# Second batch's transposes and projections moved from turn 0 into the lead, and the SyncE queue of the lead reordered

## What is computed

```python
mod = (silu(c) @ wmod).reshape(4, 6, 1, -1)
sa, ca, ga, sb, cb, gb = (mod[:, n] for n in range(6))      # ga, gb kept away from zero
h = layernorm(x) * (1 + ca) + sa
xq, xk, xv = h @ wq.T, h @ wk.T, h @ wv.T                   # 16 heads of 16
probs = softmax(xq @ xk.T)                                  # over 512 keys, per head
x = x + ga * ((probs @ xv) @ wo.T)
h = layernorm(x) * (1 + cb) + sb
x = x + gb * moe(h)                                         # 32 experts, the best 4 of each token, and a shared one
```

## Time and profile before

| | us |
|---|---|
| median of 3 runs | 596.38 |
| lowest, highest | 596.19, 599.55 |
| the profiled execution | 599.47 |
| its span, first to last instruction | 597.7 |
| TensorE busy | 560.9 (94%) |
| VectorE busy | 374.9 (63%) |
| ScalarE busy | 255.3 (43%) |
| GpSimd busy | 206.1 (34%) |

### The profile page before, as it was taken

The page is one execution under the profiler, slowest core; times in us unless marked ns, Lnnn a source line. Parts: engine busy times, 40 slices in busy tenths (PEclk is TensorE's granted clock), DMA queues, the critical chain, the costliest instruction groups (busy, mean ns, idle before and its releaser), DMA issues.

```text
span 597.7 us, 10693 instructions
## 1 busy us (share of the span) xinstructions
PE 560.9 (94%) x3102; PEld 308.7 (52%) x3103; DVE 374.9 (63%) x888; ACT 255.3 (43%) x519; POOL 206.1 (34%) x268
## 2 busy tenths in 40 slices
PE   4989999999999999999999998989998999999983
PEld 3443323233333333333343455638887898988572
DVE  6375577778679786798856469545343443442588
ACT  3112635664866648555568240123333343444000
POOL 6200000000020751207533663722665666667200
PEclk9975999999999999999999999999999999999998
DMA  6133117100221222212100688433544655540592
GB/s 228 40 110 123 27 34 218 34 7 16 68 49 37 80 82 77 44 35 82 62 1 29 222 255 249 136 91 107 157 146 137 180 161 159 166 125 18 209 404 91
DMA packets 44119, 67.18 MB, mean 112 GB/s; under 512 B 9499, under 2 KB 32420, under 8 KB 43692
## 3 DMA queue, kind: packets, MB, share of 16 engines
q1 hardware_dynamic: 31984, 45.62, 26.5%
q0 software_dynamic: 7680, 16.87, 8.1%
q10 hardware_dynamic: 4416, 4.20, 2.1%
HBM read 38.93 MB, written 27.51 MB: 111 GB/s over the span
## 4 chain that ended last, share of the span: by engine, by line
PE 83%; DVE 9%; DMA 2%; issue 2%; SPq 2%; ACT 1%; POOL 0%; ACTq 0%; DVEq 0%; POOLq 0%
PE ps L875 23%; PE ps L888 11%; PE ps L1106 9%; PE ps L972 8%; PE ps L1127 6%; PE ps L824 5%; PE ps L966 4%; PE ps L1092 3%; PE ps L846 3%; PE ps L833 3%; PE ps L901 3%; DVE max_q L1217 2%; PE ps L1117 2%; PE ps L810 2%; PE ps L931 1%
## 5 line engine op out<-in xcount | busy, mean ns | idle before, releaser
L1217 DVE TENSOR_REDUCE max_q<-ps 128x1 f32<-128x512 f32 x256 | 163.7, 684 | 73.6 <-PE ps L846 71.7
L703 ACT ACTIVATE probs<-ps 128x512 f32<-128x512 f32 x256 | 138.0, 596 | 102.1 <-PE ps L875 101.8
L846 PE MATMUL ps<-k_rows,q_rows 31*128 31x512 f32 x512 | 150.1, 681 | 1.1 <-DMA k_rows<-qk_raw 1.1
L875 PE MATMUL ps<-q_rows,k_rows 32*128 32x512 f32 x512 | 146.4, 650 | 0.9 <-DVE max_q L1217 0.9
L561 POOL DMA_INDIRECT results<-y_sb,dest x96 | 94.9, 988 | 70.3 <-ACT y_sb L752 35.2
L875 PEld LDWEIGHTS ps<-q_rows,k_rows 32*128 32x128 f32 x512 | 41.8, 186 | 70.6 <-ACT probs L703 51.1
L1106 PE MATMUL ps<-up_sb,oT 128*128 x384 | 70.8, 327 | 0.9 <-issue 0.7
L888 PE MATMUL ps<-probs,v_ext 128*32 128x512 f32 x512 | 68.2, 605 | 1.1 <-ACT probs L703 1.1
L1106 PEld LDWEIGHTS ps<-up_sb,oT 128*128 128x128 f32 x384 | 61.3, 190 | 1.9 <-issue 1.8
L1579 DVE COPY oT<-ps 128x512 f32<-128x512 f32 x48 | 33.1, 691 | 32.8 <-PE ps L1092 32.8
L1127 PE MATMUL ps<-down_sb,e_hidT 96*128 x192 | 49.8, 382 | 4.0 <-ACT e_hidT L760 4.0
(11 more groups left out here) (181 smaller groups left out, 681.9 us busy)
## 6 DMA issues: line engine op xcount, KB each, us to landing
xe<-dispatched SPq DMA_DIRECT2D x96, 129.0 KB, 2.1
comb<-results SPq DMA_DIRECT2D x16, 512.0 KB, 10.6
up_sb<-in_up SPq DMA_DIRECT2D x12, 512.0 KB, 4.7
dispatched<-pad_rows SPq DMA_DIRECT2D x33, 129.0 KB, 4.0
down_sb<-in_down SPq DMA_DIRECT2D x4, 768.0 KB, 6.7
x<-in_x ACTq DMA_DIRECT2D x4, 512.0 KB, 4.8
q_rows<-qk_raw SPq DMA_DIRECT2D x64, 32.0 KB, 1.9
k_rows<-qk_raw SPq DMA_DIRECT2D x64, 32.0 KB, 1.9
```

The costliest lines, as they stand in the source:

```text
L703: act.activation(probs[:, u % 8, :], ps[:, st_bank(t.b, g, u), :], ACT.Exp).then_inc(exp_done, 1)
L846: pe.matmul(ps[:, banks[u % len(banks)], :], q_rows[32 * i:32 * i + ONE, b % 2, g, qt * P:(qt + 1) * P], k_rows[32 * i:32 * i + ONE, b % 2 ...
L875: pe.matmul(ps[:, st_bank(b, g, n), :], k_rows[32 * i:32 * i + 32, b % 2, g, kt * P:(kt + 1) * P], q_rows[32 * i:32 * i + 32, b % 2, g, :] ...
L1217: dve.tensor_reduce(max_q[:, g % 2, qt, i:i + 1], ps[:, banks[(16 * g + n) % len(banks)], :], AXX, ALU.max).then_inc(max_done, 1)
```

## The change

In the lead, TensorE now does TP0 and TP1 of batch 1 after score n = 11 of group 0 (both named with a +), QK0+ to QK3+ after n = 3, 7, 11 and 15 of group 1, and V0+ and V1+ behind them, before it waits for the 32 maxima. ScalarE's evacuations move with them, and the normalisation of batch 1 stands before `values_out` of batch 0; the VectorE instruction that it needs (`minus_mean_over_deviation`) moves ahead of the first maxima. TP, QK and V leave table FIRST; MAX3 stands at place 24 instead of 26. On SyncE, `max_rows(lead, 3)` goes in front of the three loads, the 32 placing DMAs of batch 1 go between the two sets of three loads, and turn 0 places nothing. scoreT of unit 2 waits for V0+. `done_in` lets later code find the lead's uses under turn 0.

```diff
@@ -57,10 +57,9 @@
 
 
 
-    LEAD = ("TP0", "TP1", "QK0", "QK1", "QK2", "QK3", "V0", "V1", "MAX3")
-
-    FIRST = {"MAX0": 0, "TP0": 1, "TP1": 3, "QK0": 5, "QK1": 7, "MAX1": 8, "MOD0": 9, "MOD1": 11, "V0": (13, 15),
-             "MAX2": 16, "MODT": 17, "QK2": (19, 21), "QK3": (23, 25), "MAX3": 26, "V1": (27, 29), "NT0": 30, "NT1": 31}
+    LEAD = ("TP0", "TP1", "QK0", "QK1", "QK2", "QK3", "V0", "V1", "TP0+", "TP1+", "MAX3", "QK0+", "QK1+", "QK2+", "QK3+", "V0+", "V1+")
+
+    FIRST = {"MAX0": 0, "MAX1": 8, "MOD0": 9, "MOD1": 11, "MAX2": 16, "MODT": 17, "MAX3": 24, "NT0": 30, "NT1": 31}
 
     MIDDLE = {"MAX0": 0, "QK0": 1, "WO0": 3, "WO1": 5, "QK1": (7, 9), "MAX1": 10, "V0": (11, 13), "HT0": 14, "HT1": 15,
               "MAX2": 16, "LOG": 17, "QK2": (19, 21), "QK3": 23, "MAX3": 24, "RANK": 25, "V1": (27, 29), "NT0": 30, "NT1": 31}
@@ -90,6 +89,13 @@
                     if self.fill and places[0] >= 16:
                         half = 1 - half
                     self.take(name, half, used)
+
+    def done_in(self, lead):
+
+
+        for name, use in lead.uses.items():
+            if name.endswith("+"):
+                self.uses[name[:-1]] = use
 
     def at(self, name, place):
 
@@ -285,6 +291,7 @@
         used = [0] * len(MISC)
         lead = Turn(-1, {"pre"}, used)
         turns = [Turn(0, {"att", "pre", "mod", "next"}, used)]
+        turns[0].done_in(lead)
         for b in range(1, B):
             turns.append(Turn(b, {"att", "post", "fill"} if b == B - 1 else {"att", "pre", "post"} if b == B - 2 else
                               {"att", "pre", "post", "next"}, used))
@@ -384,12 +391,9 @@
             def turn(t):
 
                 max_rows(t, 0)
-                if t.pre:
+                if t.pre and not t.mod:
                     place_rows(t, 0, 0)
                     place_rows(t, 0, 1)
-                if t.mod:
-                    place_rows(t, 1, 0)
-                    place_rows(t, 1, 1)
                 max_rows(t, 1)
                 if t.mod:
                     modulation_out()
@@ -399,10 +403,11 @@
                 if t.pre:
                     pad(11 * t.b, 11 * t.b + 11)
                 max_rows(t, 2)
-                if t.pre:
+                if t.pre and not t.mod:
                     for c in (2, 3):
                         for g in (2, 3):
                             place_rows(t, c, g)
+                if t.pre:
                     max_rows(t, 3)
 
             sp.wait_ge(consts, 3)
@@ -412,10 +417,13 @@
             for g in range(NG):
                 for c in range(2):
                     place_rows(lead, 2 * (g // 2) + c, g)
+            max_rows(lead, 3)
             sp.dma_start(wmod[:, :, 2 * D:6 * D], wmod_in[:, 2 * D:6 * D].rearrange("(k p) n -> p k n", p=P)).then_inc(w_ld, 16)
             for w_d, w_s in ((wo, wo_sb), (gate, gate_sb)):
                 sp.dma_start(w_s[:, :, :], w_d.rearrange("(k p) n -> p k n", p=P)).then_inc(w_ld, 16)
-            max_rows(lead, 3)
+            for c in range(4):
+                for g in (c // 2 * 2, c // 2 * 2 + 1):
+                    place_rows(turns[0], c, g)
             for w_d, w_s in ((sgate, sgate_sb), (sup, sup_sb), (sdown, sdown_sb)):
                 sp.dma_start(w_s[:, :, :], w_d.rearrange("(k p) n -> p k n", p=P)).then_inc(sh_ld, 16)
             for t in turns:
@@ -725,11 +733,17 @@
                 to_hT(lead, f"TP{k}", 0)
             for c in range(4):
                 raw_qk(lead, c)
+            act.wait_ge(nmr_s, 2)
+            normalise(turns[0])
             for m in range(2):
                 values_out(lead, m)
+            for k in range(KD):
+                to_hT(turns[0], f"TP{k}", 1)
             negate_max(lead, 3)
-            act.wait_ge(nmr_s, 2)
-            normalise(turns[0])
+            for c in range(4):
+                raw_qk(turns[0], c)
+            for m in range(2):
+                values_out(turns[0], m)
             for t in turns:
                 turn(t)
             finish(fin)
@@ -870,7 +884,7 @@
                 else:
                     if b == 0 and u == 2:
 
-                        written(pe, lead, "V1")
+                        written(pe, lead, "V0+")
                     above(pe, exp_done, 64 * b + u - 2)
                 pe.matmul(ps[:, st_bank(b, g, n), :], k_rows[32 * i:32 * i + 32, b % 2, g, kt * P:(kt + 1) * P],
                           q_rows[32 * i:32 * i + 32, b % 2, g, :], start=True, stop=True, tile_position=(32 * i, 0)).then_inc(st_full, 1)
@@ -1059,9 +1073,16 @@
                 score(0, 0, n, SC + ST[0:2])
                 if n in (3, 7):
                     project_v(lead, n // 4)
+                if n == 11:
+                    for k in range(KD):
+                        tokens_to_columns(turns[0], f"TP{k}", 1)
             turn_max(lead, 3)
             for n in range(16):
                 score(0, 1, n, SC + ST[0:2])
+                if n % 4 == 3:
+                    project_qk(turns[0], n // 4)
+            for m in range(2):
+                project_v(turns[0], m)
 
             pe.wait_ge(max_done, 32)
             pe.wait_ge(ones_ld, 16)
@@ -1562,9 +1583,9 @@
             for to, of in ((iota_ef, iota_e), (base_f, base_i), (thr_f, thr_i), (tile_f, tile_i)):
                 st.did(dve.tensor_copy(to[:, :], of[:, :]))
             st.did(dve.tensor_copy(tails[:, :, :, 0], home[:, :].rearrange("p (t k) -> p t k", k=TOPK)))
+            minus_mean_over_deviation(TJ, NT, 2)
             for n in range(16):
                 score_max(0, 0, n, SC + ST[0:2])
-            minus_mean_over_deviation(TJ, NT, 2)
             for n in range(16):
                 score_max(0, 1, n, SC + ST[0:2])
             for t in turns:
```

## The result

| | before | after |
|---|---|---|
| median | 597.20 us (20 runs) | 600.75 us (20 runs) |
| lowest, highest | 594.05, 601.37 | 597.12, 603.68 |
| ratio, 95% interval | | 1.0046 (1.0027 to 1.0066) |
| profiled execution, its span | 599.47, 597.7 | 600.14, 598.4 |

The ratio makes the changed kernel 2.7 us slower (1.6 to 3.9): within 1%, but clear of zero. The forecast was +0.7. It was made on the median of the 3 runs then shown; over more runs the median of the kernel before is 0.8 higher. The two medians of the table lie 3.6 apart; I go by the ratio. The 600.75 lies outside the forecast's own range (595.5 to 598.5), inside the wide one (593 to 602), and next to the 601.2 of rival (b).

The account below looks back on a forecast made before the run. TensorE, busy 94% of the span, was taken to bound the kernel, with VectorE bounding lead group 1; +2.15 up to place 8 and -1.41 after gave +0.7 on 596.38, so 597.1 us, own range 595.5 to 598.5, wide 593 to 602.

Parts of the forecast that it names:

- rival (b): SyncE's queue: placings and 1.5 MB of weights delay place 8's maxima to about 77, 4.1 late: 601.2 us; chance 0.2.
- transposed maxima of the lead (TP0+, TP1+ cost 0): End of group 0: two transposes of 0.59 us each hide under about four VectorE maxima and cost 0.
- low clock in the lead: Group 1: the clock falls as before, 6.5 to 8.0 us at half clock, losing 3.2 to 4.0 us of work.
- places 13 to 16: Turn 0 after place 8: losing V0, they take 2 x 4.04 + 0.21 instead of 10.00 us, a gain of 1.71.
- wait for the broadcast: Place 18: VectorE arrives 1.71 us earlier and waits 1.26 for the modulation broadcast, so 1.26 is lost again.
- halves at 19 to 29: Odd places of turn 0: six moved halves give back 0.16 us each, 0.96 in all.
- the prediction's own signs: Wrong if turn 0 begins before 55, place 8 waits for `q_rows`, or pairs without a projection take clearly under 4 us.
- so it costs 0 by a small margin: SyncE's queue: maxima for place 8 land at 70.2 or 71.2, 1.7 to 2.7 us before 72.9, costing 0.
- an empty place: Turn 0: a pair holding nothing else still takes 4.04 us, its odd place 1.97, as scoreT waits for an exponential.
- Rival (a): Lead: the clock does not fall or returns at once; place 8 at 70.7 as before, the rest -1.4: 595.0 us; chance 0.2.
- The term for turn 0: Turn 0 to the start of place 8: 15.37 us at full clock instead of 21.17, a gain of 5.80.
- rival (c): Turn 0: an emptied place gives back all its work, halves worth 1.1 each, 5.4 us more: 591.7 us; chance 0.1.

Follow-up runs that it names:

- after, again: The changed kernel without edit, profiled a second time and timed in pairs with the kernel before: 599.88 us, ratio 1.0050.
- e5: e1 plus two unread matmuls behind score 15 of group 0, where TensorE would wait for VectorE: 594.99 us, ratio 0.9969 to the kernel before.
- e1: The changed kernel with turn 0's group 0 maxima sent before the last eight placing DMAs and the three loads: 598.05 us, ratio 1.0008 to the kernel before.
- e2: The changed kernel with only the three shared-expert weight loads moved behind turn 0's group 0 maxima: 597.77 us, ratio 1.0004 to the kernel before.
- e8: The changed kernel, SyncE's order kept, plus two unread matmuls behind score 15 of group 0: 601.94 us, ratio 1.0080 to the kernel before.
- e6: e4 plus unread matmuls behind score 15 of group 0 and after scores 11 and 15 of group 1: 592.92 us, ratio 0.9922 to the kernel before.
- e4: The changed kernel with only TP0, TP1, QK0, QK1 moved and maxima sent before the shared expert's weights: 599.41 us, ratio 1.0032 to the kernel before.
- e3: The kernel before with nine unread matmuls added among the lead's scores to keep TensorE busy: 594.30 us, ratio 0.9945 to the kernel before.

## Why the prediction was right or wrong

Times of events are given behind the first score here, since the first score itself moves by some tenths. The forecast's are less 25.26.

| step | forecast | after | after, again |
|---|---|---|---|
| transposed maxima of the lead (TP0+, TP1+ cost 0) | 12.16 | 12.16 | 12.16 |
| low clock in the lead | 6.5 to 8.0 | 3.4 | 6.8 |
| turn 0 begins | 32.2 | 29.5 | 31.0 |
| TensorE ready for place 8 | 47.6 | 44.5 | 45.9 |
| maxima for place 8 landed | 44.9 to 45.9 | 46.9 | 48.3 |
| wait at place 8 | 0 | 2.4 | 2.4 |
| cost of the low clock behind it | 0 | 1.6 | 1.6 |
| places 13 to 16 | -1.71 | -0.94 | -0.94 |
| wait for the broadcast | 1.26 | 0 | 0 |
| halves at 19 to 29 | -0.96 | -0.96 | -0.96 |

The last four rows are read between the matmuls of MOD0, MOD1, MODT and the transposes of batch 2: from the start of place 8 to MOD0 4.99 and 4.98 (3.35 before, 70.65 to 74.00), from MOD1 to MODT 14.01 in both (14.95 before), from MODT to the transposes 28.37 in both (29.33 before).

**The size** was in the range and the class (within 1%) was right; the sum was 2 us too low, and this was not noise. That the time fell into the range is owed to the room left for rival (b), not to the sum. And by two of the prediction's own signs it was wrong: place 8 waited for `q_rows` in both profiles, and turn 0 began before 55 in the first (54.26; 55.99 in the second).

**The step that failed** is SyncE's "so it costs 0 by a small margin". Both sides of the margin of 1.7 to 2.7 us were off by 1 to 3. TensorE came 3.1 and 1.7 earlier: its 16.1 us in the lead are 15.6 at full clock (e5), the low clock cost it 1.55 and 3.0 instead of the 3.6 in the sum (29.50 and 30.95 against e5's 27.95), and from turn 0 to place 8 it took 15.0 instead of 15.4. The maxima came 1.0 and 2.4 later: the last placings and `sgate` were issued more slowly (5.34 and 1.92 us instead of 4.96 and 0.5), and SyncE stood idle until QK0+ was evacuated, for 0.3 us in the first profile and 1.45 in the second (its first placing starts at 43.98 there), so that the same low clock that holds TensorE in the lead holds SyncE's queue as well; I had let that queue run from the end of the loads. Of the forecast's two landings the later one, behind `sdown`, was the right kind (0.5 and 0.8 behind it). The mechanism of rival (b), head of line, was right; the point from which it decides was reached by small errors and not by the 12.6 us of landing at which I had priced it.

A misread row stands behind this too. The earlier trace rows put the wait of 1.36 us of an empty pair into the even place (291.27), behind 1.07 for the odd one; the prediction counted it to the odd place, at 1.97. So TensorE is ready for place 8 about 0.9 us sooner than an empty place 7 was priced, and for that 0.9 a late DMA costs nothing. A slower first pair of places (4.5 us in e1, 54.05 to 58.57) hides half of it in the 15.0.

**And the stall's consequence was missed.** Rival (a) let TensorE wait for the DMA at place 8 at no further cost, though the same text argued that the clock falls where TensorE waits. The runs put wait and low clock together at about 3 us in the changed kernel (e1 and e2 against after; 2.4 + 1.6, less the 0.9 for the exponential), and at 5.7 with the lead at full clock (e8 against e5).

**The clock.** That it would fall in the lead again was right in three of the four profiles in which the lead was as changed and not filled (after, again, e2; not e1). The term for turn 0, 5.80 gained up to place 8, took 20 us of low clock in the kernel before for typical; its second profile had 17 and was 1.5 us earlier at the end of place 8. That is the second part of the miss, and it is why the pair of first profiles shows +0.7 (span) to +1.3 (M) where the runs show +2.7. Put together, in the two pairs of profiles the lead took 5.2 and 7.4 longer (forecast 7.95), turn 0 up to the end of place 8 2.2 and 2.0 less (forecast 5.80), and the rest up to batch 2 1.8 and 1.2 less (forecast 1.41).

**The broadcast.** There was no wait at place 18, by two small misses that add up. SyncE's timeline and VectorE's of the changed kernel:

```profile
88.66 0.50 SPq L383 DMA_DIRECT2D mod_b<-modulation  x1
```

```profile
100.86 0.75 DVE L1289 TENSOR_TENSOR wo_g<-wo_sb,gate_b 128x256 f32<-128x256 f32 x2
```

It landed after 11.8 us, at 100.5, 0.4 before it was needed. And places 13 to 16 gave 0.94, not 1.71, since places 15 and 16 gave nothing: 90.60 to 95.54 is 4.94, the same as 88.87 to 93.81 before. The chain at place 16, after:

```profile
91.67 1.79 PE ps L889 x4
93.46 0.88 PE ps L860 x4
```

and before:

```profile
91.00 1.06 PE ps L875 x4
92.06 0.55 PE ps L846 x4
```

With V0 gone, its 1.06 us has turned into a longer wait at place 16. There the first score of the next batch waits, by its semaphore value, for all maxima of this one and not for those of three units before; I read this from the code, and no run tested it.

**What held:** an empty place (4.03 to 4.04 us a pair, in e6 and after), so that 16 us of moved TensorE work gave only few back; the halves, 0.96 as forecast; the transposes under VectorE's maxima; and rival (c) did not occur.

## What to carry to other kernels

Work that a dependence already covers is not worth moving: price a place by what it still takes when empty, not by what is taken out. A queue with one order is part of the path of the last DMA in it; when work moves forward, look which small, urgent transfer now stands behind it. And where an engine's clock can fall behind a stall, as here, the stall costs its length and then the slow stretch, so a margin of 2 us that hangs on the clock is none.

## What the runs showed of the hardware

The granted clock fell behind gaps of TensorE that were shorter than the slow stretches that followed. In all eight profiles whose lead was not filled, TensorE stands idle for 1.86 or 1.87 us at the end of group 0, waiting for VectorE, and in seven of them the clock fell within this gap or up to 1.3 us behind it. In the eighth (e1) it did not. TensorE's timeline of the changed kernel's second profile, of e1, and of e4, where such a gap stands before turn 0 and the clock fell 1.0 behind it:

```profile
37.20 0.38 PE L868 MATMUL ps<-ident,max_q 128*16 128x128 f32 x1 [1.87 <-DVE max_q L1238]
```

```profile
36.91 0.28 PE L871 MATMUL ps<-ident,max_q 128*16 128x128 f32 x1 [1.87 <-DVE max_q L1241]
```

```profile
50.88 0.70 PE L890 MATMUL ps<-q_rows,k_rows 32*128 32x512 f32 x2 [1.87 <-DVE max_q L1237]
```

It fell as well at each of the three waits for the maxima (2.4, 2.4 and 4.1 us), and at that place in no profile without the wait. But a gap is not needed: in e2 it fell at 95.4 with TensorE busy without a break. And once low it stays low while TensorE is busy: at 37.7 to 40.0 in the kernel before it stands at 0.50 with TensorE busy for 2.30 of 2.30 us. Whether the gap alone or also the single matmuls at VectorE's pace in front of it let the clock fall, no run separates; e5 filled the gap only, and that was enough in its one profile.

Two (e5) to nine (e3) unread matmuls in such gaps and around them kept it at 1.00 through the lead in all four kernels that had them, and three of these were faster by ratio than the same kernels without: 0.9945 against 1 (e3), 0.9922 against 1.0032 (e6, e4), that is 3 and 7 us; and 0.9969 against 1.0008 (e5, e1), where the intervals overlap. The fourth is e8, which then waited. In the lead the low clock, once it had fallen, lasted 3.4 and 6.8 us with the added projections behind it (after), and 17 and 20 us with scores alone (before).

Each placing DMA of 32 KB took 0.63 us of SyncE's time (8 in 5.01), and one of the 2 KB of maxima nearly as much (4 in 2.19), so 32 placings hold the queue for 20 us.
